# Writing the 0/1 matrix early in a step of VectorE, and fetching the row set ahead of the sums on TensorE

## The reference

```python
h_fwd = h @ W_forward.T                      # h = layernorm(x), 6250 nodes x 256
h_rev = h @ W_reverse.T
messages = h_fwd[src] * direction[:, 0:1] + h_rev[src] * direction[:, 1:2]
scores = leaky_relu(einsum('ef,hf->eh', messages, attn), 0.2)   # 4 heads
exp_scores = exp(scores - max)
sum_exp = segment_sum(exp_scores, dst)
norm = exp_scores / (sum_exp[dst] + 1e-10)
out[:, hd] = segment_sum(messages * norm[:, hd], dst)           # 200000 edges
```

## Time and profile before

| | us |
|---|---|
| median of 3 runs | 2604.11 (2593.95 to 2609.36) |
| the profiled execution | 2600.62 |
| its span, first to last instruction | 2598.8 |
| PE / DVE / ACT / POOL busy | 2048.6 / 1607.9 / 825.9 / 1681.9 |
| mean granted clock of TensorE | 0.874 |

### The profile page before, as it was taken

The page is one execution under the profiler, slowest core; times in us unless marked ns, Lnnn a source line. Parts: engine busy times, 40 slices in busy tenths (PEclk is TensorE's granted clock), DMA queues, the critical chain, the costliest instruction groups (busy, mean ns, idle before and its releaser), DMA issues.

```text
span 2598.8 us, 57994 instructions
## 1 busy us (share of the span) xinstructions
PE 2048.6 (79%) x14057; PEld 1456.5 (56%) x14058; DVE 1607.9 (62%) x4968; ACT 825.9 (32%) x2950; POOL 1681.9 (65%) x1797
## 2 busy tenths in 40 slices
PE   6478778877887787788778777877876459999970
PEld 6255555555555555555555555555556458888870
DVE  6566565666666666656565665656558736666657
ACT  5132223222222322232222223222336324344335
POOL 7777777777777777777777777777716733333327
PEclk9599889988988898898889889988975579999995
DMA  5222222222222222222222222222232675665657
GB/s 173 78 63 62 59 62 62 62 57 60 60 58 60 60 60 58 60 60 59 58 59 60 58 60 60 60 58 60 61 112 83 219 229 198 201 201 193 197 171 255
DMA packets 185170, 255.17 MB, mean 98 GB/s; under 512 B 61158, under 2 KB 129159, under 8 KB 184868
## 3 DMA queue, kind: packets, MB, share of 16 engines
q0 software_dynamic: 55104, 124.66, 19.4%
q1 hardware_dynamic: 127572, 127.75, 15.8%
q10 hardware_dynamic: 2448, 2.26, 0.3%
HBM read 216.63 MB, written 38.77 MB: 98 GB/s over the span
## 4 chain that ended last, share of the span: by engine, by line
PE 41%; DVE 23%; issue 14%; DVEq 13%; ACT 3%; SPq 2%; DMA 2%; POOL 1%; ACTq 0%; POOLq 0%
PE p_hot L962 33%; DVEq L865 7%; PE p_win L873 4%; DVEq L1649 3%; DVE shared L980 3%; DVE token_rows L1036 2%; DVE hot_ex L1019 2%; DVE rows L1047 2%; SPq L1224 2%; DVE p_y L1856 1%; ACT rows L928 1%; PE p_h L1792 1%; DVE hid_t L1828 1%; PE p_y L1802 1%; DVE second L1836 1%
## 5 line engine op out<-in xcount | busy, mean ns | idle before, releaser
L239 POOL DMA_INDIRECT rows<-node_table,index x1419 | 1339.5, 944 | 487.7 <-issue 420.6
L962 PE MATMUL p_hot<-token_rows 128*128 128x408 bf16 (+1 forms) x7344 | 1271.2, 334 | 4.4 <-issue 0.2
L962 PEld LDWEIGHTS p_hot<-token_rows 128*128 128x128 bf16 x7344 | 722.8, 100 | 508.5 <-issue 33.2
L873 PE MATMUL p_win<-hot_ex,msg 128*65 128x64 f32 x3136 | 265.1, 248 | 328.8 <-DVE hot_ex L1019 328.8
L914 ACT ACTIVATE p_part<-rows,attr_all 128x64 f32<-128x64 f32 x1568 | 387.7, 299 | 216.6 <-DVE rows L1047 212.5
L873 PEld LDWEIGHTS p_win<-hot_ex,msg 128*65 128x65 f32 x3136 | 250.5, 163 | 359.1 <-issue 326.2
L980 DVE TENSOR_TENSOR shared<-shared,p_win 65x64 f32 x784 | 170.9, 218 | 395.0 <-issue 309.6
L1036 DVE TENSOR_TENSOR token_rows<-key,p_dve 128x1152 bf16<-128x1152 f32 (+1 forms) x288 | 356.0, 1275 | 0.0
L928 ACT ACTIVATE rows<-p_hot,third 128x136 f32<-128x136 f32 x144 | 53.9, 374 | 784.1 <-PE p_hot L962 784.1
L1658 POOL DMA_INDIRECT expert_rows<-ys,back x104 | 102.9, 990 | 291.9 <-DVE ys L1861 215.7
L1047 DVE SCALAR_TENSOR_TENSOR rows<-p_hot,third,rows 128x136 f32<-128x136 f32 x288 | 102.7, 357 | 191.7 <-ACT rows L928 168.2
(11 more groups left out here) (248 smaller groups left out, 1519.6 us busy)
## 6 DMA issues: line engine op xcount, KB each, us to landing
shared<-in_w SPq DMA_DIRECT2D x120, 512.0 KB, 4.1
rows<-node_table,index POOLq DMA_INDIRECT x1419, 3.8
xs<-dispatched SPq DMA_DIRECT2D x104, 129.5 KB, 4.2
shared<-expert_rows SPq DMA_DIRECT2D x12, 896.0 KB, 8.2
key<-hot_keys SPq DMA_DIRECT2D x48, 192.0 KB
token_rows<-in_x SPq DMA_DIRECT2D x7, 896.0 KB, 10.9
token_rows<-in_x SPq DMA_DIRECT2D x7, 768.0 KB, 9.0
out<-shared SPq DMA_DIRECT2D x6, 896.0 KB, 7.9
```

Source lines behind the costliest of these rows:

```text
L239: pool.indirect_dma_start(out=rows[:, s, k, :], out_offset=None, in_=table, in_offset=bass.IndirectOffsetOnAxis(ap=index[:, s, k:k + 1], a ...
L873: last = pe.matmul(psum[0:MSG, u * HEADS * W:(u + 1) * HEADS * W], msg[:, k, :], weighted[:, k, :, :].rearrange("p h w -> p (h w)"), start ...
L962: last = pe.matmul(p_hot[:, s % 2, 0:width * ROW], onehot[:, s % 2, gr, :], parts[:, gr:NT:GP, m, :], start=(gr == 0 and m == 0), stop=(gr ...
```

## The change

In the step of VectorE the call of `build_hot` for the chunk two on moves from behind `extra_windows` to the top, ahead of the wait for the gathered rows. In the step of TensorE the call of `fetch` for the chunk two on moves from behind the sums to the top, ahead of the waits for the messages. The two functions themselves, LEAD, the buffers and all waits in them stay. `keep_others` and `keep_first` stay in their places.

```diff
@@ TensorE
                 def step(c, s, it, loaded):
+                    if coming(s, it, LEAD):
+                        fetch(*coming(s, it, LEAD))
                     pe.wait_ge(msg_ready, c + 1)
                     pe.wait_ge(val_ready, c + 1)
                     after(pe, added, UPC * c)
...
                         pe.nop()
-                    if coming(s, it, LEAD):
-                        fetch(*coming(s, it, LEAD))
@@ VectorE
                 def step(c, s, it, loaded):
                     v = s % 2
+                    if coming(s, it, LEAD):
+                        build_hot(*coming(s, it, LEAD))
                     all_rows(dve, c, s, it)
                     dve.wait_ge(attr_ready, c + 1)
                     after(dve, msg_ready, c)
...
                     extra_windows(c, s, loaded[s])
-                    if coming(s, it, LEAD):
-                        build_hot(*coming(s, it, LEAD))
                     if coming(s, it, 1):
                         keep_others(*coming(s, it, 1))
```

## The result

The changed kernel takes 2527.0 us (median of 4 runs, 2526.2 to 2528.7) against 2606.4 (2594.0 to 2609.4) beside it: a ratio of 0.971, 95% interval 0.968 to 0.974. Forecast were 2536 and a range of 2522 to 2574. The profiled executions have spans of 2598.8 and 2525.4, 73.4 us apart.

A forecast was written before the change was run, and what follows sets the result against it. VectorE and TensorE taking turns bound the kernel, GpSimd second. Last gather 47.6 us earlier plus 22.5 from the tail, 70.1, less 2 for the reload: 68 saved, 2532.6, as a median 2536; range 2522 to 2574.

The forecast's parts named there:

- The alternation and the two waits: Edge loop: VectorE and TensorE take turns; VectorE's waits of 1.72 and 1.69 us go, turn 37.55 to about 36.3.
- GpSimd's pace: Edge loop: 29 gathers of 1.253 us become the bound, 36.3 us a turn; last gather at 1847.9, 47.6 us earlier.
- The tail: From the last gather's start to the node stage: 14.5 us instead of 37.0, saving 22.5.
- reload of `token_rows`: SyncE's reload runs beside the last eight gathers: 2 us lost, ends 0 and 10.
- The TensorE path: Serial path through TensorE and VectorE in the edge loop: 34.9 us a turn (34.2 to 35.7), under GpSimd's 36.3.
- 9.0 + 3F: Length in us of that serial path per turn, F being one fetch, taken as 8.65.
- 36.06: Longest turn in us that still allows the 70 us gain; needs a mean fetch of at most 9.02.
- The margin: Distance of the TensorE and VectorE path from costing any gain: 1.1 us a turn.
- partial rival: Slow fetches behind idling make a turn 35.2 to 36.5 us, up to 37.2; 45 us saved, 2559; chance 0.14.
- The clock: Slower rival: low-clock fetches delay TensorE's sums from a mean fetch of 9.52 us; 2637 at 9.75; chance 0.08.
- The key: Key tile's DMA for next turn's chunk 0: no wait to 2.9 us late; nothing taken.

The follow-up runs named there:

- two half changes: Kernel before with only VectorE's early build_hot: 2861.9 us against 2595.3; with only TensorE's early fetch: 3359.4 against 2595.3.
- warmed kernel: Kernel before plus 28 matmuls in TensorE's step 1 of each of the 47 middle turns, filling its wait: 2535.6 us against 2595.3, ratio 0.977.
- first four experiments: Only VectorE's half, only TensorE's half, kernel before with extra matmuls, kernel before with four gathers fewer: 2861.9, 3359.4, 2535.6, 2609.8 us against 2595.3.

## Why the prediction was right

**The alternation and the two waits.** Right: a turn of 36.3 as forecast, L1047 without its wait for L928, no 6.5 us gap, L987 (now L989) waiting for gathers. The two half changes show that neither move does it alone.

**GpSimd's pace.** Right: the last gather forecast at 1847.9, measured 1845.0, since one takes (1845.0 - 101.46) / 1394 = 1.251 us and not 1.253.

**The tail.** Right: 14.5 us forecast, and 2 for the reload of `token_rows` beside the last gathers; 16.5 measured. The chain of waits at the end shows it:

```profile
1841.25 5.90 DMA rows<-node_table,index
```

The last gather of chunk 194 needed 5.9 us from its start until VectorE went on, against a median landing of 3.9; the reload had begun at 1838.0. Inside the loop the same takes about 4.1 us (1015.81 to 1019.90). That the reload is the cause is an inference from the time at which it runs; no run leaves it out. `head_max` was forecast near 1864 and came at 1861.46. The sum, 68 us, measured 73.4: 2.9 from the gathers' interval and 2.4 from behind the loop. Of the 9 us between 2536 and 2527.0 the rest is the 3.5 us by which the profiled execution lay under the median before; after, the two are the same (2527.18 and 2527.01). The ends 2522 and 2550 of the forecast's own range were worked from 2532.6 and not from 2536.

**The TensorE path** was the term that I sized too low. It shows before VectorE has caught up with the gathers, which it does at 674.7 (first wait of L989 for a gather). Until then the matrices for the next turn's chunk 0 start from

```profile
147.55 2.48 DVE L1036 TENSOR_TENSOR token_rows<-key,p_dve 128x1152 bf16<-128x1152 f32 x2
...
646.83 2.48 DVE L1036 TENSOR_TENSOR token_rows<-key,p_dve 128x1152 bf16<-128x1152 f32 x2
...
674.74 0.72 DVE L989 TENSOR_TENSOR part<-rows,p_attr 128x544 f32<-128x544 f32 x1 [0.86 <-DMA rows<-node_table,index]
```

These are 14 turns in 499.3 us, 35.66 us each, where I had 34.9. The rows of TensorE say why:

```profile
147.10 2.01 PE L873 MATMUL p_win<-hot_ex,msg 128*65 128x64 f32 x16 [2.96 <-DVE hot_ex L1021]
148.96 9.32 PE L962 MATMUL p_hot<-token_rows 128*128 128x408 bf16 x51
...
169.77 8.63 PE L962 MATMUL p_hot<-token_rows 128*128 128x408 bf16 x51 [1.15 <-issue]
...
182.30 1.16 PE L873 MATMUL p_win<-hot_ex,msg 128*65 128x64 f32 x16 [2.96 <-DVE hot_ex L1021]
184.16 10.31 PE L962 MATMUL p_hot<-token_rows 128*128 128x408 bf16 x51 [0.69 <-DVE token_rows L1036]
```

One fetch in three, the one behind the idle stretch, takes 9.3 to 10.3, the two others 8.62 and 8.63, and the loads at the loop's head cost 0.9 to 1.15 and not 0.45. Over these two turns the mean fetch is 9.02 us, exactly the value up to which the prediction's 9.0 + 3F leaves the whole gain. That 35.66 and not 36.06 came out is luck: the rest of the path takes 8.6 us and not 9.0, as a sum adds about 0.95 us between two fetches and not 1.13, and signal and keep are shorter too. The margin was 0.4 us and not 1.1. The turn lies within the partial rival's 35.2 to 37.2, so its mechanism was at work; it cost nothing as long as the turn stayed under 36.06. Its chance of 0.14 was too small.

**The clock.** The prediction had the low clock as a danger of the new order. It was as much the price of the old one: 1.2 us a turn by the rows of before, and the warmed kernel shows that without it GpSimd no longer waits. I had not named this in the prediction. It is not what the changed kernel gained by, whose sum behind the gap is as slow as before (1.93 us); there the path no longer holds up VectorE. The spread of the runs fits, though it was not tested: 15 us before, 2.5 us after (7 us before on the chip of the first four experiments).

**The key.** Not late. The trace has no landing for it, but in the turn above its transfer is issued at 1001.61, and the matrix that needs it starts at 1007.48 with no idle time ahead of it. L1036 idles only at the loop's head (about 1.8 us, 41 times as issue and 7 times put down to L962). The prediction's bound of 1.9 us for an issue was a mean of seven; the longest of them took 3.0.

## What to carry to other kernels

When two engines hand work to each other once a step, look in the timeline for the same idle gap on both; move the producer's part to the head of its step and the consumer's ahead of whatever waits for the current step, both or neither. Before pricing the gain find the third engine's pace, because the gain ends there, and add what its lead was worth at the end of the loop. A gap in TensorE's work can cost more than its length (here 1.2 us of slow work behind 6.5 us of idling): if it can't be closed, cheap matmuls in it may buy much of what a new order does, here 2.3% of 2.9%.

## What the runs showed of the hardware

- TensorE's granted clock fell behind gaps of 2.96 us too, and not at the same point of the work behind them. In these stretches (length, busy us of each engine with instructions, clock, DMA) it is 0.50 for one sum and 1.00 for the next, which is followed by 0.55 in the fetch:

```profile
147.10:149.00 1.90, 1.90 (x17) 1.87 (x18) 1.75 (x4) 1.23 (x6) 1.29 (x3) 0.50 0.24 52
182.30:184.00 1.70, 1.16 (x16) 1.02 (x16) 1.55 (x3) 1.03 (x5) 1.09 (x2) 1.00 0.17 41
184.20:188.00 3.80, 3.80 (x13) 1.72 (x14) 2.25 (x6) 2.23 (x11) 2.88 (x4) 0.55 0.26 56
```

- The same program takes about 2600 us on some chips and 3600 on others, with single matmuls 2.1 us apart inside the loop. I had not expected that and can't say where it comes from.
- On the chips of 2600 us a GpSimd gather of 128 rows of 544 bytes kept its 0.94 to 0.95 us, 1.25 with its issue, in both kernels, the half changes and the warmed kernel.
